# Three small moves in a fused attention and feed-forward kernel: the scalar engine's last rotary split, one matmul between two score rounds, and GpSimd's layer-norm steps among its causal masks

## The reference: what is computed

```python
x = L0_attn_x                                # 8 batches x 512 tokens x 512
xn = layernorm(x)
s = attention(xn, Wq, Wk, Wv, Wo)            # 16 heads of 32, RoPE on q and k, causal softmax
h = bitlinear(xn, w_fc); h = gelu(h)         # w_fc: 2048 x 512, ternary weights
g = silu(bitlinear(h, w_proj))               # w_proj: 512 x 2048, ternary weights
return x + s * g
# bitlinear: layer_norm over the last axis, then a product with sign(round(w/gamma))*gamma
```

## Time and profile before

| | |
|---|---|
| median of three runs | 1146.66 us |
| time of the profiled execution | 1146.66 us |
| span of its profile | 1144.9 us |
| TensorE busy | 1106.4 us, 97% |
| VectorE / ScalarE / GpSimd busy | 75% / 69% / 44% |
| TensorE's granted clock | full speed in all 40 slices |

### The profile page before, as it was taken

The page is one execution under the profiler, slowest core; times in us unless marked ns, Lnnn a source line. Parts: engine busy times, 40 slices in busy tenths (PEclk is TensorE's granted clock), DMA queues, the critical chain, the costliest instruction groups (busy, mean ns, idle before and its releaser), DMA issues.

```text
span 1144.9 us, 20202 instructions
## 1 busy us (share of the span) xinstructions
PE 1106.4 (97%) x7548; PEld 605.3 (53%) x7548; DVE 854.7 (75%) x1596; ACT 789.7 (69%) x1508; POOL 504.3 (44%) x915
## 2 busy tenths in 40 slices
PE   4989899999999999999999999999999999999997
PEld 3555654458444574446644475445844467444763
DVE  6987977798657986489756987479865898658864
ACT  4787884588825888179762788448882688727984
POOL 2035351463615635175433745156361553526433
PEclk9999999999999999999999999999999999999999
DMA  8491002920019101371016410192011910145111
GB/s 311 157 109 42 1 3 65 109 80 18 7 39 150 38 2 30 45 122 38 3 29 81 86 38 4 29 110 84 11 14 39 144 38 2 30 56 74 38 37 40
DMA packets 52610, 67.30 MB, mean 59 GB/s; under 512 B 9376, under 2 KB 34336, under 8 KB 52000
## 3 DMA queue, kind: packets, MB, share of 16 engines
q1 hardware_dynamic: 52512, 66.02, 31.1%
HBM read 31.98 MB, written 8.40 MB: 35 GB/s over the span
## 4 chain that ended last, share of the span: by engine, by line
PE 78%; DVE 7%; DMA 5%; ACT 5%; SPq 2%; POOL 1%; issue 1%; DVEq 0%; ACTq 0%
PE banks L549 16%; PE banks L423 15%; PE banks L594 11%; PE banks L656 7%; PE banks L675 7%; PE banks L528 5%; PE banks L605 5%; PE banks L440 5%; DMA stacks<-split_buf 4%; ACT banks L856 2%; SPq L346 2%; PE banks L535 2%; DVE arena L1120 2%; DVE mix L1144 1%; PE banks L454 1%; POOL split_buf L1338 1%
## 5 line engine op out<-in xcount | busy, mean ns | idle before, releaser
L856 ACT ACTIVATE banks<-banks,mix,scl 128x384 f32<-128x384 f32 (+2 forms) x384 | 248.7, 652 | 29.7 <-POOL mix L1353 27.2
L1144 DVE TENSOR_REDUCE mix<-banks 128x1 f32<-128x512 f32 (+3 forms) x352 | 216.7, 636 | 26.8 <-PE banks L535 21.1
L549 PE MATMUL banks<-xT,fcT 128*128 128x512 f16 x1024 | 228.8, 379 | 6.0 <-ACT xh_buf L820 5.9
L594 PE MATMUL banks<-proj_ones,arena 128*128 128x256 f16 (+1 forms) x1536 | 213.4, 273 | 0.3 <-DVE mix L1072 0.3
L1338 POOL TENSOR_TENSOR split_buf<-xr_buf,split_buf 128x512 f16<-128x512 f32 x64 | 74.4, 1184 | 296.1 <-ACT split_buf L797 296.1
L879 ACT ACTIVATE arena<-banks,scl 128x1280 f32<-128x1280 f32 x128 | 162.9, 1328 | 29.2 <-PE banks L656 26.2
L1344 POOL TENSOR_TENSOR xh_buf<-xh_buf 128x512 f32<-128x512 f32 x120 | 152.4, 1270 | 65.5 <-ACT xh_buf L820 64.3
L423 PE MATMUL banks<-xT,qkT 128*128 128x512 f16 x768 | 168.7, 379 | 0.0
L549 PEld LDWEIGHTS banks<-xT,fcT 128*128 128x128 f16 x1024 | 97.8, 98 | 127.0 <-ACT xh_buf L820 15.1
L594 PEld LDWEIGHTS banks<-proj_ones,arena 128*128 128x128 f16 x1536 | 141.3, 97 | 36.4 <-issue 0.6
L1353 POOL TENSOR_SCALAR mix<-mix,scl 128x1 f32<-128x1 f32 (+1 forms) x288 | 76.3, 265 | 181.3 <-DVE mix L1144 180.3
(11 more groups left out here) (163 smaller groups left out, 1465.3 us busy)
## 6 DMA issues: line engine op xcount, KB each, us to landing
stacks<-split_buf SPq DMA_DIRECT2D x192, 128.0 KB, 5.4
out_dram<-arena SPq DMA_DIRECT2D x32, 256.0 KB, 2.0
xr_buf<-in_L_attn_x_dram SPq DMA_DIRECT2D x7, 1024.0 KB, 8.5
resid<-in_L_attn_x_dram SPq DMA_DIRECT2D x28, 256.0 KB, 5.4
stacks<-in_L_ffn_w_fc_dram SPq DMA_DIRECT2D x1, 4096.0 KB, 26.3
arena<-in_L_ffn_w_proj_dram SPq DMA_DIRECT2D x1, 4096.0 KB, 14.6
mix<-norm_row SPq DMA_DIRECT2D x8, 256.0 KB, 5.0
xr_buf<-in_L_attn_x_dram SPq DMA_DIRECT2D x4, 256.0 KB, 3.7
```

Source lines behind the costliest of these rows:

```text
L549: mm = pe.matmul(banks[:, UP_BANKS[f % NUB], :], fcT[:, c, f * P:(f + 1) * P], xT[:, part, c, :], start=(c == 0 and part == 0), stop=(c == ...
L594: mm = pe.matmul(banks[:, DOWN_BANKS[h % 3], 0:cols.stop - cols.start], hid[:, part, f, t * P:(t + 1) * P], proj_ones[:, f, cols], start=( ...
L856: mm = nc.scalar.activation(block, block, ACT.Exp, scale=col(EXP_SCALE), bias=exp_bias[:, i, h0 + k:h0 + k + 1], accum_out=row_sum[:, i, h ...
L1144: nc.vector.tensor_reduce(row_max[:, i, h0:h0 + n], scores_of(r), AX_X, ALU.max).then_inc(max_ready, 1)
```

## The change

Three places change. The order of TensorE's, VectorE's, ScalarE's and GpSimd's streams changes in them, and no instruction is added or taken away.

```diff
-LN_AHEAD = 6
-LN_AFTER_HEADS = (3, 4, 5, 6)
-RSTD_AFTER_HEAD = 7
+RSTD_AFTER_HEAD = 10
@@
-LEAD = (0, 4, 12, 17, 20)
+LEAD = (0, 4, 11, 17, 20)
@@ ScalarE, inside `for f in range(FC)`
-                    if f == 0:
+                    if f == (0 if first else 2):
                         split_rotated(3)
                     if f >= 1:
                         square(f - 1)
@@ GpSimd
                 steps = normalise_steps(b + 1)
-                for _ in range(0 if last else LN_AHEAD):
-                    next(steps)
@@ GpSimd, in mask(g), after the two mask instructions of head GH * g + k
-                        if GH * g + k in LN_AFTER_HEADS and not last:
-                            next(steps)
+                        if not last:
+                            next(steps, None)
                         if GH * g + k == RSTD_AFTER_HEAD:
```

## The result

The changed kernel took 1154.09 us (median of five runs, 1152.52 to 1155.75), beside 1146.71 us for the kernel before (five runs, 1146.58 to 1148.08). The ratio is 1.0061, with a 95% interval of 1.0047 to 1.0077: slower by 0.6%, where 0.5% was forecast. The time lies inside the stated range of 1148.0 to 1154.5 by 0.4 us, and two of the five runs (1154.55 and 1155.75) lie above it. The profiled execution took 1155.67 us (span 1154.0), so its profile has 9.1 us more than the profile before, about 1.6 us more than the median of its runs has.

The account below looks back on a forecast made before the run. TensorE, busy for 97% of the span, was taken to bound the kernel. The terms summed as 1146.66 - 1.3 + 2.6 + 4.3 = 1152.3 us, slower by 0.5%, with a range from 1148.0 to 1154.5.

Parts of the forecast that it names:

- Part 1: Up projection, batches 1 to 7: casts behind Gelu 2 remove 7.0 us of waits, add 5.7 at tile 4: -1.3 us.
- The bound of -2: Up projection: lower bound in us for moving the casts, if a small wait of batch 1 at a later tile went too.
- The rival in which ScalarE catches up: Up projection: casts fit ScalarE's gaps, no wait at tile 4, full -7.0 us gained; 1144.0 us, chance 0.06.
- Part 2: Score rounds: tile 1 scaled after round 4 makes the 25th matmul wait 0.37 us in seven batches: +2.6 us.
- Part 3: GpSimd's norm steps one per head, reciprocal root after head 10: head 11's mask late for `weigh(2, 0)`, +4.3 us.
- the second piece: At `weigh(2, 0)`: normalise on VectorE slows head 10's masks and the power by 0.37 us in batches 0 to 6.
- masks without contention: Rival at `weigh(2, 0)`: head 11's mask only 0.21 us late, 1.7 us in all; 1149.7 us, chance 0.17.
- A missing wait: Rival: no new wait at the 25th matmul (1149.7 us), at head 11 (1148.0) or at both (1145.4); chance 0.17.
- The full lock: Rival: each of head 10's two mask instructions waits for a full normalise instruction, 9.4 us; 1157.4 us, chance 0.08.

Follow-up runs that it names:

- e1: Kernel before with only the casts of pair 3 moved behind Gelu 2 in batches 1 to 7: 1144.64 us, ratio 0.9975.
- e8: Kernel before with one cast of pair 3 behind `square(1)` and one behind `square(2)` in batches 1 to 7: 1139.29 us, ratio 0.9931.
- e2: Kernel before with only LEAD[2] at 11, and with it tile 1 scaled one round later: 1150.12 us, ratio 1.0024.
- e4: Kernel before with LEAD[2] at 11, but tile 1 still scaled after round 3's maxima: 1147.10 us, ratio 1.0000.
- e5: Kernel before with only the reciprocal root moved, from after head 7 to after head 10: 1148.76 us, ratio 1.0014.
- e6: Kernel before with only the norm steps moved, one per head from head 0: 1150.45 us, ratio 1.0027.
- e9: Kernel before with three norm steps ahead of the masks, then one after each of heads 0 to 6: 1146.99 us, ratio 1.0002.
- e7: Changed kernel with W_o's load issued ahead of the two residual loads in batch 1: 1153.67 us, ratio 1.0058 to the kernel before.

## Why the prediction was right, and which terms were mis-sized

The direction came out, and so did the size: 1152.3 forecast, 1154.09 measured. Three of its mechanisms stood where they were put. That the number lies within the range is partly luck: a wait of 3.2 us and one of about 1 us were missed, two of the terms that were there were too dear by 0.7 and 0.6, and the time is 0.4 us below the range's upper edge.

- **Part 1, forecast -1.3, measured -2.0.** The wait that went was worth 177.15 - 7 x 24.31 = 7.0, as forecast. The new one started at 7.74 and not 7.80, and cost 0.71 and not 0.82 of the stretch. Tile 4 started at 6.91 without a wait, so it is 0.83 late by starts, and 0.12 of this comes back: in batches 1 to 7 of the kernel before, batch 1 too, tile 7's first matmul starts 0.35 us behind its neighbour in place of 0.22, and in the changed kernel it doesn't. The bound of -2 named just that small later wait. This term is 5.0 instead of 5.7. e1 shows it alone. The rival in which ScalarE catches up fell for this order. Its prize was real, though: e8, in another order, took 6.4 of the 7.0 us. That rival's sum of 1144.0 had a slip: it took 1.7 for part 3, and with the forecast's own 4.3 it is 1146.6, no faster than before.
- **Part 2, forecast +2.6, measured 7 x 0.38 = 2.7; e2 alone +2.8 by its ratio.** e4 shows the reason too: VectorE's order, not the matmul.
- **Part 3 at `weigh(2, 0)`, forecast 7 x 0.58 + 0.21 = 4.3, measured 7 x 0.50 + 0.2 = 3.7.** Both pieces are seen apart: 0.20 a batch for the order (e5), and 0.37 on GpSimd with normalise beside it. That the second piece has the forecast's size is in part luck, since half of it fell on the power and not on the masks.
- **What was missed: "no row of the waits has TensorE waiting for a mask in a way that counts", so "nothing is gained" was all that was said of heads 0 to 7.** A list of waits of the kernel before tells who waits now; it can't tell who will wait. Two slow steps (the powers) went from ahead of all masks to between them, and I added up their effect for head 11 and not for head 7. It costs 0.46 us in seven batches, 3.2 us (e6 alone: +0.46). What should have warned me were GpSimd's times in the kernel before, at the masks of head 5 in batch 3, beside the gate sum on VectorE (POOL's timeline, before):

```profile
571.14 1.53 POOL L1378 TENSOR_SCALAR_AFFINE_SELECT arena<-arena 128x256 f32<-128x256 f32 x2 [0.41 <-ACT arena L879]
572.64 0.63 POOL L1310 TENSOR_TENSOR norm_c<-ln 128x4 f32<-128x4 f32 x1
573.34 0.76 POOL L1378 TENSOR_SCALAR_AFFINE_SELECT arena<-arena 128x256 f32<-128x256 f32 x2
```

  Two masks took 1.53 in place of 0.77 and a small product 0.63 in place of 0.20: the gate sum already cost GpSimd 1.2 us there, with slack behind it. With a full power of 1.04 in that place there was none. By the rows of the changed kernel, head 7's first mask ended 0.44 us behind the time at which TensorE could have started. The slower power makes 0.44 and the slower masks 0.73, so either alone at full speed would have cleared the wait or nearly so. That the contention is needed is argued from these durations. Shown is that the steps alone bring the wait (e6), and that it is gone when the second power stands behind head 2 (e9).
- **W_o in batch 1, forecast nothing.** The sum named SP's queue for the stores and the next tokens, but not what stood behind the norms in batch 1. It costs about 1.2 us in some executions; e7 removes 0.9 of it, and the rest goes with the late norm rows.
- **Slack that held.** VectorE's idle time ahead of its rotary products fell from 91.8 us in all (L1120) to 78.4 (L1118). The forecast had it fall from 9 to about 5 in a batch, and it fell less: at the row that the forecast read, from 9.09 to 8.45. Neither the later pair 3 nor, in batches 2 to 7, the later norms held TensorE: in batches 5 to 7 the four numbers -0.23, 0.38, 0.50 and 0.46 add up to 1.11 of the measured 1.12.

Of the rivals, masks without contention (1149.7) fell by e5 and the 2.11 against 1.74. A missing wait fell: all three were there. The full lock (part 3 at 9.4) fell at the place for which it was worked out: head 10's pair lost 0.19 there (0.96 against 0.77), not 1.10. At the gate sum a pair of masks lost 0.73. Taken apart instruction by instruction (batch 3 of the changed kernel), both places show the two engines taking turns. Alone, masks start 0.36 us apart. Beside the gate sum the second mask and the power behind it start 0.83 apart, and the gate sum's last two instructions 0.81, in place of 0.67. Beside normalise the second mask and the power start 0.56 apart, and normalise's instructions 0.55, in place of 0.46. So both engines lose, and GpSimd loses more beside the longer VectorE instruction. The Trainium skill (SBUF — State Buffer, "SBUF: two separate sides") speaks of an exclusive lock for VectorE and GpSimd, held for a whole instruction; the turns agree with it, and the forecast's worst case, in which each mask loses a whole normalise instruction on top, doesn't. No run here varies the VectorE instruction at one place.

The errors partly cancelled: -0.7 in part 1 and -0.6 at `weigh(2, 0)`, against +3.2 and +1.2 that were missed. In the profiled execution 0.6 of the start-up comes on top, and 0.5 of batch 2 goes off.

## What to carry to other kernels

When steps are moved on an engine, follow its queue to every instruction that another engine waits for, not only to those where someone waits today, and price each step at what its kind takes in rows where the same neighbour runs (here a power took 1.04 us alone and 1.48 beside the gate sum). A block that is longer than the gap of one round should be cut at its instructions and put into two gaps: the same two casts gave 0.25% behind Gelu 2, 0.4% behind `square(1)` and 0.7% in a gap each. And where a position is computed from a table, a change to the table moves more than its own instruction: here the whole cost of part 2 came with the scaling that followed.

## What the runs showed of the hardware

- GpSimd's 128x4 power took 1.04 us alone, 1.20 where it started in the middle of VectorE's normalise (float32, one tensor read) and 1.48 where it started in the middle of the gate sum (two tensors read). A pair of 128x256 masks took 0.77, 0.96 and 1.50 to 1.60. I had expected the power to be nearly untouched, since it moves only 4 elements per partition. What also counts is who starts first: in the kernel before, the power started 0.02 us ahead of normalise in seven batches and took 1.05 beside it, and the loss fell on the masks behind it and on normalise.
- The issue of two residual loads (256 KB each) in batch 1 took SP about 0.91 us in nine of the twelve profiles and 2.60 (e7), 2.97 (e6) and 3.90 (the changed kernel) in three, for the same instructions. A slow issue isn't tied to this place: behind the start-up every profile has one to five issues of over 1.5 us. In the kernel before, one store of the norms in batch 3 took 2.98. Nothing in the rows around them says why.
- The order that gives the same wait in every batch gave the steadier profile: 136.38 to 136.39 us per batch in batches 2 to 7, where the kernel before had 135.10 to 136.89. Its up stretches, with stalls that end when stack DMAs land, make 1.3 us of that spread (25.09 to 26.36).
